# Attention on one core: a projection part of an even step is issued after the first score of the odd step behind it

## What is computed

```python
qkv = x @ qkv_w + qkv_b                      # (2, 2048, 3, 16, 32)
attn = softmax(einsum('bnhd,bmhd->bhnm', q, k) * 32 ** -0.5)
out = einsum('bhnm,bmhd->bnhd', attn, v).reshape(b, n, c)
```

## Time and profile before

| | |
|---|---|
| time before, median of 3 runs | 3881.74 us (3879.18 to 3888.47) |
| the profiled execution's own time | 3886.65 us |
| its span, first to last instruction | 3884.5 us |
| self-attention's steps (first to last score) | 109.5 to 2187.2 us of the span |
| PE busy | 3494.0 us (90%) |
| DVE busy | 2552.2 us (66%) |
| ACT busy | 1735.6 us (45%) |
| POOL busy | 2085.9 us (54%) |
| mean granted TensorE clock | 0.947 |

### The profile page before, as it was taken

How to read it: one execution, slowest core, us unless ns; L and a number is a source line. 1 busy time by engine, 2 the same in 40 slices (tenths; PEclk the granted TensorE clock), 3 DMA queues, 4 the chain that set the end, 5 groups by cost and what they waited for, 6 DMA issues and landing times. The chain is left out here.

```text
span 3884.5 us, 51792 instructions
## 1 busy us (share of the span) xinstructions
PE 3494.0 (90%) x18133; PEld 2290.6 (59%) x18134; DVE 2552.2 (66%) x4514; ACT 1735.6 (45%) x3066; POOL 2085.9 (54%) x1039
## 2 busy tenths in 40 slices
PE   7999999999999999999999578787859889999885
PEld 5455455454554554545543156766749778888774
DVE  6777777777777777777775156777634655556666
ACT  2455555555555555555555332232213433333342
POOL 1789898889898988888988600211110001100112
PEclk9999999999999999999998788998869899999998
DMA  6321312222213132222100211221122233323332
GB/s 216 102 54 59 94 51 87 68 63 83 74 56 104 47 91 69 63 83 68 56 23 4 88 61 44 79 79 55 44 106 81 97 105 109 103 90 104 120 115 97
DMA packets 190735, 309.76 MB, mean 80 GB/s; under 512 B 25609, under 2 KB 72329, under 8 KB 190490
## 3 DMA queue, kind: packets, MB, share of 16 engines
q1 hardware_dynamic: 164330, 238.58, 19.7%
q0 software_dynamic: 15072, 45.89, 3.4%
q10 hardware_dynamic: 11088, 22.02, 1.7%
HBM read 197.23 MB, written 61.33 MB: 67 GB/s over the span
## 5 line engine op out<-in xcount | busy, mean ns | idle before, releaser
L463 DVE TENSOR_REDUCE sa_part_max<-sa_mx 128x1 f32<-128x512 f32 x2048 | 1281.5, 679 | 542.4 <-PE sa_mx L574 538.3
L426 ACT ACTIVATE sa_prob<-sa_sc 128x512 f32<-128x512 f32 x2048 | 1121.8, 595 | 823.3 <-PE sa_sc L620 780.7
L247 POOL TENSOR_TENSOR sa_quad_sum<-sa_quad_sum,sa_prob 128x1024 f32<-128x1024 f32 x512 | 1208.8, 2397 | 7.3 <-ACT sa_prob L426 7.3
L574 PE MATMUL sa_mx<-sa_k_stack,sa_q_stack 96*128 96x512 f32 x2048 | 966.0, 474 | 27.8 <-DVE sa_part_max L463 15.9
L620 PE MATMUL sa_sc<-sa_q_stack,sa_k_stack 98*128 98x512 f32 x2048 | 865.4, 424 | 8.1 <-ACT sa_prob L426 8.1
L247 POOL TENSOR_TENSOR sa_quad_sum<-sa_prob 128x1024 f32<-128x1024 f32 x256 | 616.6, 2431 | 253.8 <-ACT sa_prob L426 253.8
L574 PEld LDWEIGHTS sa_mx<-sa_k_stack,sa_q_stack 96*128 96x128 f32 x2048 | 389.6, 190 | 377.9 <-issue 205.8
L620 PEld LDWEIGHTS sa_sc<-sa_q_stack,sa_k_stack 98*128 98x128 f32 x2048 | 388.9, 190 | 318.1 <-ACT sa_prob L426 273.4
L1809 PE MATMUL ex_h<-ex_xT,ex_w 128*128 128x384 f32 (+2 forms) x2688 | 469.0, 330 | 80.8 <-DVE ex_xT L1711 28.6
L1809 PEld LDWEIGHTS ex_h<-ex_xT,ex_w 128*128 128x128 f32 x2688 | 451.6, 196 | 105.9 <-issue 70.9
L589 PE MATMUL sa_pv<-sa_prob,sa_v 128*32 128x512 f32 x4096 | 501.7, 608 | 0.7 <-ACT sa_prob L426 0.7
(11 more groups left out here) (199 smaller groups left out, 3374.4 us busy)
## 6 DMA issues: line engine op xcount, KB each, us to landing
ex_w_in<-in_L_ffn_w_dram SPq DMA_DIRECT2D x130, 512.0 KB, 4.4
sa_xT<-xT SPq DMA_DIRECT2D x57, 1024.0 KB, 5.1
sa_q_stack<-sa_hilo SPq DMA_DIRECT2D x372, 64.0 KB, 2.0
sa_k_stack<-sa_hilo SPq DMA_DIRECT2D x360, 64.0 KB, 2.0
ex_xg<-rows POOLq DMA_DIRECT2D x54, 256.0 KB, 3.3
rows<-sa_empty SPq DMA_DIRECT2D x48, 257.0 KB, 3.7
ex_rows<-rows POOLq DMA_DIRECT2D x8, 1542.0 KB, 7.5
sa_prob<-in_x_dram ACTq DMA_DIRECT2D x8, 1024.0 KB, 7.2
```

Source lines behind the costliest of these rows:

```text
L247: pool.tensor_tensor(quad_sum[:, i % 2, heads, :], so_far, prob[:, k, heads, :], ALU.add).then_inc(quad_ready, 1)
L426: act.activation(prob[:, kt % 4, j, :], sc[n % 2][:, :], ACT.Exp, scale=SCALE).then_inc(prob_ready, 1)
L463: dve.reduce_max(part_max[:, q, j, k:k + 1], mx[n % 3][:, :], AX_X).then_inc(max_read, 1)
L574: pe.matmul(mx[n % 3][:, :], q_stack[0:QK, j, at:at + P], k_stack[0:QK, g // NQ % 2, j, k * BANK:(k + 1) * BANK], start=True, stop=True).t ...
```

## The change

The part of an even step leaves its place at the end of that step and is issued in the odd step that follows, behind that step's first max and score. Parts of odd steps stay where they are. Nothing is added or removed.

```diff
                         score(g, kt, i)
+                        if i == 0 and kt % 2 == 1 and (g, kt - 1) in PART_AT:
+                            project_part(*PART_AT[g, kt - 1])
                         if i == 1 and kt % 2 == 0:
                             burst(g, kt)
                         if i == 2 and kt == T - EARLY and g + 1 < CHUNKS:
                             transpose_shift(g + 1)
-                    if (g, kt) in PART_AT:
+                    if kt % 2 == 1 and (g, kt) in PART_AT:
                         project_part(*PART_AT[g, kt])
```

## The result

The changed kernel took 3918.79 us (median of 4 runs, 3913.15 to 3922.38) against 3881.28 (3879.18 to 3888.47) for the kernel before: ratio 1.0092, 95% interval 1.0074 to 1.0110. The forecast was 3912, in a range of 3895 to 3923, and slower. The profiled executions differ by less than the medians: the span went from 3884.5 to 3915.6 us, 31.1 more. The profiled execution of the changed kernel took 3917.74 us, where the forecast had 3917 for it.

A forecast was written before the change was run, and what follows sets the result against it. PE sets self-attention's pace, held in a latency loop with ACT. Added to 3881.74 us, 28.1 (chunks 1 to 27), 1.4 (chunk 0) and 0.7 (chunks 28 and 29), together 30, give 3912 us; range 3895 to 3923.

The forecast's parts named there:

- The loop between PE and ACT: In self-attention, PE's scores wait for ACT's exponentials to free banks while ACT waits for scores; neither engine is full.
- runs of 3 and 3 scores: Between PE's holes, scores are cut 3 and 3 instead of 2 and 4; 0.23 us more a pair with both parts.
- The price of a held score: A PE score waiting for its bank's exponential costs 0.15 us of waiting and 0.10 of weight load, 0.25 in all.
- the rival with both loads ready: Weight loads of both parts in a pair are ready behind held scores: only 5 us more, 3887; chance 5%.
- DVE hides the loss in steps 2 to 5: DVE's unbroken run sets the pace there; steps 2 to 5 together pay 0.12 us in place of 2 x 0.23.
- the part no longer waits for L457: Step 4's part waits for L457; score 0 of step 5 now goes ahead, gaining nothing since max 3 waits for DVE.
- The head start of DVE: Rival: in steps 3 to 5 DVE starts 0.6 us earlier, saving 16 us: 3866; chance 7%.
- The lock between L472 and POOL: Rival: in step 12, L472 meets POOL's additions and waits, 98 to 118 us more, about 4020; chance 5%.
- The sum: Self-attention: chunks 1 to 27 28.1 us, chunk 0 1.4, chunks 28 and 29 0.7; together 30 us more.
- Waits for the exponential should be more in number: Sign in the profile after: PE's waits for ACT's exponential increase in number; no size given.

The follow-up runs named there:

- halved parts: Kernel before, with each even step's part cut in two, the second half issued behind score 1 of the odd step: 3842.5 us, ratio 0.9877.
- that run: Kernel before, with two needless 128x514 additions put behind POOL's additions of the third quad of every chunk: 4043.5 us, ratio 1.0407.

## Why the prediction was right, point by point

- **The loop between PE and ACT.** Right, and shown from both sides: runs of 3 and 3 scores cost 0.23 to 0.25 us a pair, 4 and 2 cost nothing against 2 and 4, and 2, 2, 2 and 2 save 0.26.
- **The price of a held score, 0.15 + 0.10.** Right. The interval over a moved q part is 1.44 for 1.43 forecast. A load that itself carries the wait starts when the wait ends, and the part's load comes behind it, as the weight loads after show; the 5 us of the rival with both loads ready, which the prediction drew from the Trainium skill (TensorE: Matmul & The Clock Gate, Part 2, step 1), did not come.
- **DVE hides the loss in steps 2 to 5.** Right: 0.13 us for the forecast 0.12, and the half of the change in steps 2 and 4 alone cost 3.9 us in chunks 0 to 27. That the part no longer waits for L457 gained nothing, as said.
- **The head start of DVE.** Excluded for this change, since the part stands between the two maxima: DVE idles 0.64 there. With the part one score later it comes, 0.61 us a chunk.
- **The lock between L472 and POOL.** Not met; the gap opened 0.17 earlier, as reckoned (0.2). Its price was under-estimated, 156 us for 98 to 118: steps 12 and 13 grew by the 4.0 us foreseen, but the lower clock behind the wait, and what it costs in steps 14 and 15, was not thought of.
- **The sum.** In chunk 0 1.6 us for 1.4, in chunks 1 to 27 29.4 for 28.1, behind them 0.8 for 0.7: 31.85 for 30 in the profile. The medians are 37.5 apart, but the interval of the ratio, 29 to 43 us, holds the 31.1 of the spans. The time of an execution goes with its mean granted clock: the kernel before, beside the experiments, took 3878 to 3885 us at 0.949 and 3889 to 3896 at 0.945. At 0.947 it took 3886.1 to 3890.0 in six executions, and the changed kernel 3917.74, 28 to 32 more. This speaks for the other 6 us being scatter; since those executions were not timed beside it, it doesn't show it.
- **Waits for the exponential should be more in number.** Wrong by the view that counts them. In the window of the earlier trace rows the waits by releaser after read:

```profile
ACT sa_prob L426 <- PE sa_sc L620: 547.6, 453, 2.8
...
PEld sa_sc L620 <- ACT sa_prob L426: 205.0, 610, 0.4
```

They are fewer (610 for 618) and longer in total (205 for 177 us). The view also counts the shorter waits of a load behind a part and of the fourth score of a run. The scores that are held in full, recorded with 0.50 us, did become more: 358 for 248 in this window. In each of chunks 1 to 27 they are twice as many as before in steps 1, 3, 7, 9 and 11 (two for one), and one as before in step 5, under DVE's run. So the mechanism was right and the sign named for it was a bad one.

## What to carry to other kernels

Where two engines hand two buffers back and forth, work to be slipped in belongs where the buffers run out, ahead of the instruction that would wait, not behind it; count how many instructions go freely after a hole (here two) and put a piece of other work after each such run, in smaller pieces if need be. One place further for the same parts turned a loss of 0.8% into a gain of 0.5%, so read the start times on both sides of the new place rather than the busy share, which was 90% in both kernels. And look for what lies close to a gap of another engine before anything moves there.

## What the runs showed of the hardware that I had not expected

An instruction of DVE on 128x16 elements that takes 0.18 us alone took 3.62 us beside POOL's additions, and did not get in where one POOL instruction followed another. With halved parts POOL had been idle ahead of it for 0.52 us or more in chunks 0 to 27, but for 0.32 in chunk 11, and it ran in 0.17 or 0.18 in all of them. That two microseconds of idle time on POOL carry 156 us of this kernel is in no view of busy time: it shows only in the duration of L472 in chunks 28 to 30.

A wait of PE of some 3 us was followed by a lower granted clock, 0.82 in the mean of steps 14 and 15 for 1.00 before, so that each such wait cost 5.25 us. With the clock, the same steps went from 7.9 to 9.9 us in that run, and chunk 31 from 58.0 to 63.4 us over all runs: more than several of the effects that the experiments were built to tell apart.
